# A four-layer conditioned stack on one core: the setup stage is spread over the first attention and the gate stage, and the norms of two attentions move one step

## What is computed

```python
# layer 0: 16 heads of 64
mod = silu(c) @ W_mod + b_mod                 # six rows of 256 per sequence: shift, scale, gate, twice
x = x + g_msa * attention(layernorm(x) * (1 + sc_msa) + sh_msa)
x = x + g_mlp * (gelu(modulated(layernorm(x)) @ W1 + b1) @ W2 + b2)
# layer 1: 16 heads of 16; rmsnorm, q and k normed and rotated by positions, SwiGLU
mod = c @ ada_w.T + ada_b
# layer 2: 16 heads of 16; layernorm, rotary, gelu MLP, then a gate:
mod = silu(c) @ film_w.T + film_b
x = x + gelu(v_) * tanh(g_) @ tg_out_w.T + tg_out_b
# layer 3: low-rank weights made from the condition
h = gelu(layernorm(c) @ W1 + b1)              # 64 x 256
w = h @ W2 + b2                               # 64 x 8192: four factors of 256 x 8 per sequence
y = gelu((x @ a1) @ bb1.T); out = x + (y @ a2) @ bb2.T
```

## Time and profile before

| what | value |
|---|---|
| time, median of 3 runs | 2367.48 us (2367.0 to 2367.68) |
| the profiled execution: its own time / its span | 2364.86 us / 2363.1 us |
| PE busy | 2005.7 us (85%) |
| DVE busy | 1455.1 us (62%) |
| ACT, POOL busy | 968.7 us (41%), 835.4 us (35%) |
| mean granted TensorE clock | 0.946 of full |

### The profile page before, as it was taken

The page is one execution under the profiler, slowest core; times in us unless marked ns, Lnnn a source line. Parts: engine busy times, 40 slices in busy tenths (PEclk is TensorE's granted clock), DMA queues, the critical chain, the costliest instruction groups (busy, mean ns, idle before and its releaser), DMA issues. The chain is left out here.

```text
span 2363.1 us, 41380 instructions
## 1 busy us (share of the span) xinstructions
PE 2005.7 (85%) x15274; PEld 1565.9 (66%) x15274; DVE 1455.1 (62%) x2120; ACT 968.7 (41%) x1594; POOL 835.4 (35%) x759
## 2 busy tenths in 40 slices
PE   4829999999999799867787679997877877998998
PEld 4618878878887577646565567774655656777775
DVE  1236655656566455468888856775777774554554
ACT  0024434434444566534454433332333345664332
POOL 0041111211011344456665723345656572443000
PEclk9959999999999999978999989998998999999999
DMA  7120000000000100010000000001000000000001
GB/s 301 55 74 2 2 2 1 1 2 1 1 1 10 49 0 0 0 41 2 0 0 0 1 25 0 0 1 36 1 0 0 0 2 27 0 0 32 5 0 72
DMA packets 19519, 44.28 MB, mean 19 GB/s; under 512 B 3200, under 2 KB 11200, under 8 KB 18176
## 3 DMA queue, kind: packets, MB, share of 16 engines
q1 hardware_dynamic: 19392, 42.48, 5.1%
HBM read 36.18 MB, written 6.29 MB: 18 GB/s over the span
## 5 line engine op out<-in xcount | busy, mean ns | idle before, releaser
L1223 DVE TENSOR_TENSOR Glb<-Gfb,Ghb 128x512 fp32r<-128x512 f32 x176 | 168.2, 964 | 101.6 <-ACT Ghb L1176 100.0
L523 POOL TENSOR_TENSOR Tm<-Dv,MOD 128x512 f32<-128x512 f32 x96 | 111.3, 1179 | 298.6 <-DVE Dv L580 208.0
L633 PE MATMUL bank<-HH,W1b 128*128 128x512 f32 x448 | 183.8, 410 | 13.2 <-PEq L1493 6.9
L633 PE MATMUL O<-Ghb,W2b 128*128 128x512 f32 x352 | 144.1, 409 | 54.0 <-DVE Glb L1223 52.4
L634 PE MATMUL bank<-HL,W1b 128*128 128x512 f32 x448 | 177.2, 396 | 0.0
L635 PE MATMUL bank<-HH,W1b 128*128 128x512 f32 x448 | 176.9, 395 | 0.0
L1378 PE MATMUL bank<-WQKa,HH 128*128 128x512 f32 x256 | 101.4, 483 | 78.3 <-DVE HL L588 63.6
L653 POOL TENSOR_TENSOR spare<-RT 128x1 f32<-128x1 f32 x48 | 9.5, 197 | 446.0 <-DVE RT L644 446.0
L512 POOL TENSOR_TENSOR XS<-Tm 128x512 f32<-128x512 f32 x48 | 70.5, 1469 | 245.6 <-ACT Tm L478 245.6
L635 PE MATMUL O<-Ghb,W2b 128*128 128x512 f32 x352 | 138.4, 393 | 0.0
L634 PE MATMUL O<-Glb,W2b 128*128 128x512 f32 x352 | 137.8, 392 | 0.0
(11 more groups left out here) (244 smaller groups left out, 5470.0 us busy)
## 6 DMA issues: line engine op xcount, KB each, us to landing
w<-l_w_dram SPq DMA_DIRECT2D x4, 2048.0 KB, 26.7
wm<-w_mods_dram SPq DMA_DIRECT2D x6, 768.0 KB, 12.1
X<-xT_dram SPq DMA_DIRECT2D x4, 1024.0 KB, 36.3
out_dram<-XO SPq DMA_DIRECT2D x8, 512.0 KB, 2.7
W2b_f<-l_w_dram SPq DMA_DIRECT2D x11, 256.0 KB, 5.0
WQK_f<-l_wqk_dram SPq DMA_DIRECT2D x8, 256.0 KB, 7.1
W1b_0f<-l_w_dram SPq DMA_DIRECT2D x8, 256.0 KB, 3.5
b2r<-l_b2r_dram SPq DMA_DIRECT2D x1, 1024.0 KB, 7.7
```

The source lines that it names most:

```text
L523: nc.gpsimd.tensor_tensor(Tm[:, k].rearrange("p (b t) -> p b t", t=T), Dv[:, k].rearrange("p (b t) -> p b t", t=T), m, ALU.mult).then_inc( ...
L633: nc.tensor.matmul(out, w_lo_ap, x_hi, start=first, stop=False)
L1223: nc.vector.tensor_tensor(Gl[m % gb][:], gf, Gh[m % gb][:].bitcast(F32), ALU.subtract).then_inc(g_lo.h, 1)
```

## The change

1. **The setup block is gone.** Constants, x (chunk by chunk) and the modulation weights (one layer at a time, in one buffer) are loaded in the block of attention 0. Layer 0's modulation is made there as before, between the norms of chunks 0 and 1. Layers 1 and 2 are made with the condition as the stationary side: two halves of 64 sequences side by side, then a copy (ACT), transposes (PE) and the store (DVE), around the first two steps.
2. **The low-rank weights are made in the gate block** (`Hyper`): in chunks 0 to 4, after the steps m = 1 and m = 3, a slot of work is put into the lists of PE, ACT and DVE. SP loads the low-rank weights in 8 parts of 1 MB, writes the factors out and only then reads them back. The gate's chunks are all written out, without a loop.
3. **attention12**: each part of the norm of chunk c + 2 moves to an earlier step of chunk c.

```diff
--- before.py
+++ after.py
 attention0, sync:
+                        for out, src in small:
+                            sp.dma_start(out, src).then_inc(d_in.h, 16)
+                        x_chunk(sp, 0)
+                        mod_weights(sp, 0)
+                        x_chunk(sp, 1)
                         st.weights.load(sp, 0)
...
                         st.weights.load(sp, 1)
+                        x_chunk(sp, 2)
+                        sp.wait_ge(m_ps.h, m_ps.at(2))
+                        mod_weights(sp, 1)
                         st.weights.load(sp, 2)
+                        x_chunk(sp, 3)
+                        sp.wait_ge(m_ps.h, m_ps.at(3))
+                        mod_weights(sp, 2)
+                        for c in range(4, NCH):
+                            x_chunk(sp, c)
 attention0, tensor:
+                def mod_products(pe, l):
+                    pe.wait_ge(m_w.h, m_w.at(32 * (l + 1)))
+                    for k in range(DH):
+                        for n in range(2):
+                            nc.tensor.matmul(O2[n * B:(n + 1) * B, 0, :], (cT if l == 1 else cS)[:, k, :], wm[:, k, n * 512:(n + 1) * 512],
+                                             start=(k == 0), stop=(k == DH - 1), skip_group_check=True)
+                    for k in range(DH):
+                        last = nc.tensor.matmul(O2[0:B, 1, :], (cT if l == 1 else cS)[:, k, :], wm[:, k, 1024:1536],
+                                                start=(k == 0), stop=(k == DH - 1), skip_group_check=True)
+                    last.then_inc(m_ps.h, 1)
...
+                        step(0, 0, 0, 2, first=True)
+                        mod_transposes(pe, 1)
+                        pe.wait_ge(m_done.h, m_done.at(6))
+                        mod_products(pe, 2)
+                        step(0, 1, 0, 2, first=True)
+                        mod_transposes(pe, 2)
+                        st.weights.ready(pe, st.weights.all())
                         chunks(pe, steps(step, lambda c: None))
 feed_forward, gate:
+                        if hyper:
+                            hyper.sync(sp)
                         nxt.loads(sp)
...
                                 last.then_inc(g_used.h, 1)
+                                if hyper:
+                                    hyper.tensor(pe, c, m)
...
-                        chunks(pe, body)
+                        chunks(pe, body, gate)
 class Hyper, tensor:
+                    for k in range(DH):
+                        for q in range(2):
+                            last = nc.tensor.matmul(S2[q * B:(q + 1) * B, 0, :], self.hT[:, k, :], self.W2[n % 3][:, q, k],
+                                                    start=(k == 0), stop=(k == DH - 1), skip_group_check=True)
 class Hyper, scalar (slots 2 to 5; slots 0 and 1 have a sqrt, a copy and two gelus):
+                    act.wait_ge(l3_ps.h, l3_ps.at(n + 1))
+                    nc.scalar.activation(self.AsT[n % 2][:], S2[:, 0, :], ACT.Copy).then_inc(l3_cp.h, 1)
 attention12, scalar:
-                            if t == (1 if more else 3):
-                                f, cc, pp = late(fr, nf, c, p, more)
-                                f.act_hh(act, cc, pp)
-                            if more and t == 3:
-                                f, cc = early(fr, nf, c, more)
-                                f.act_sqh(act, cc)
...
+                            f, cc = early(fr, nf, c - 1 if tail else c, more)
+                            if t == 1:
                                 f.act_square(act, cc)
-                            if more == 2 and tail:
-                                fr.act_rstd(act, c + 1)
+                            if t == 2:
+                                f.act_sqh(act, cc)
+                            if t == 3 and more:
+                                f.act_rstd(act, cc)
+                            if tail and more:
+                                f.act_hh(act, cc, 1 - p)
 attention12, gpsimd:
+                            if t == 1:
+                                f.pool_ss(pool, cc)
+                            if t == 2:
+                                f.pool_sql(pool, cc)
                             if t == 3 and more:
-                                f.pool_sql(pool, cc)
-                            if more == 2 and t == 0:
-                                fr.pool_h(pool, c + 1, 1 - p)
+                                f.pool_h(pool, cc, p)
```

More of the change, by code:

```diff
@@ L621, in x_there, with x_loaded, chunks @@
             pass
-        def chunks(eng, body):
+        def x_loaded(eng, c):
+            if isinstance(c, int) and c < 2:
+                eng.wait_ge(x_in[c].h, x_in[c].at(16 * DH))
+        def chunks(eng, body, unrolled=False):
+            if unrolled:
+                for c in range(NCH):
+                    body(c, c % 2, 2 if c < NCH - 2 else NCH - 1 - c)
+                return
             with eng.Fori(0, NCH // 2 - 1) as j:
@@ L814, in _ @@
-                        pe.wait_ge(d_in.h, d_in.at(16))
+                        pe.wait_ge(c_set.h, c_set.at(2))
+                        fr.pe_mean(pe, 0)
+                        pe.wait_ge(f_d.h, fr.at(f_d, 1))
+                        fr.pe_var(pe, 0)
+                        pe.wait_ge(m_w.h, m_w.at(32))
+                        pe.wait_ge(c_sil.h, c_sil.at(1))
+                        for h in range(2):
+                            for m in range(6 * h, 6 * h + 6):
+                                for k in range(DH):
+                                    last = nc.tensor.matmul(BK[h][:, (m % 6) * B:(m % 6) * B + B], wm[:, k, m * P:(m + 1) * P], cS[:, k, :],
+                                                            start=(k == 0), stop=(k == DH - 1))
+                            last.then_inc(m_ps.h, 1)
@@ L938, in step @@
                                 wt.high(act, 4 if j == 0 else wt.all())
-                        for j in range(2):
-                            step(0, j, 0, 2, first=True)
+                        mod_copy(act, 1)
+                        step(0, 0, 0, 2, first=True)
+                        st.weights.high(act, 4)
+                        mod_copy(act, 2)
+                        step(0, 1, 0, 2, first=True)
                         chunks(act, steps(step, lambda c: None))
@@ L1202, in body @@
                                     wt.high(act, 1)
-                        chunks(act, body)
+                        chunks(act, body, gate)
                     @block.vector
@@ L1258, in body @@
                                 residual_dve(dve, c, l, G_M, bcol_out, O2)
-                        chunks(dve, body)
+                        chunks(dve, body, gate)
                     @block.gpsimd
@@ L1748, in step @@
                                 ol(tt - 1, prev)
[L1749 to L1752 removed]
+                            f, cc = early(fr, nf, c - 1 if tail else c, more)
+                            if t == 1:
+                                f.dve_d(dve, cc)
+                            if t == 3 and more:
+                                f.dve_norm(dve, cc)
+                            if tail and more:
+                                f.dve_hl(dve, cc, 1 - p)
                         def residual(c, more):
```

519 lines of the change are left out of this document (265 added, 254 removed).

## The result

| | before | changed |
|---|---|---|
| median of 4 runs | 2367.24 us | 2256.68 us (2252.96 to 2259.85) |
| ratio, 95% interval | | 0.9532 [0.951, 0.9554] |
| profiled execution: own time / span | 2364.86 / 2363.1 us | 2252.96 / 2251.1 us |
| PE busy, mean granted clock | 2005.7 us, 0.946 | 1965.9 us, 0.957 |

What follows compares the result with a forecast made beforehand. By stage, PE was taken to bound the gate and nothing in the middle attentions, where it waited 63.6 us for HL. 2364.9 - 111 + 34 - 50 = 2238, plus 2.6 for the median: 2240 us, range 2210 to 2276.

Steps and rivals of the forecast that it cites:

- Term 1: Head of the program, up to attention 0's third step of heads: removing the serial prelude saves 111 us (bounds 104 to 116).
- three main points: Head: DVE and ACT start at 13.3 us, first projection at 44.8, third step of heads at 78.
- The price of half-products side by side: Modulation products of layers 1 and 2: halves run together, 0.93 us per 512-column product, 3.7 us per layer.
- Term 2: Gate: low-rank weight slots add 19.4 us of PE work and 14.6 of waits, +34 us (bounds 24 to 52).
- The rule on weight loads: Gate: loads overlap products only for another row group, so column halves run one after the other: +52, total 2258.
- the row: Profile row of line 736: 64 half-records in 3.71 us, so halves run together; gate +34, total 2240.
- Term 3: Attentions of layers 1 and 2: moving norm parts earlier removes PE's wait for HL, -50 us (bounds 26 to 70).
- about 39.3, so 3.2 a chunk: Layer 1's attention: a turn falls from 42.5 to about 39.3 us, a gain of 3.2 us per chunk.
- The first rival: Attentions: DVE's later output tile makes PE idle in the tail instead; gain 0 to 10 us, total about 2285; 8%.
- cost 2 in each layer: First chunk of layers 1 and 2: DVE stands still for chunk 1's HL where PE did, costing 2 us each.
- DVE and POOL stop each other: Attentions: modulation, norm, HL and residual, moved together, each could lose 1 us; 42 us less gain, total 2282; 7%.
- Feed-forward 2 and low rank: Feed-forwards and low-rank layer: unchanged, so 0 us difference.

Runs made afterwards that it cites:

- part 3 alone: Kernel before with only the attention of layers 1 and 2 as changed, setup and gate as before: 2337.35 us, ratio 0.9869.
- the fastest kernel: Changed kernel with gate slots one step later, first norm earlier in both layers, tile chain first in layer 2 only: 2209.02 us, ratio 0.9334.

## Why the prediction was right, and where it was not

The measured median lies inside the range, with the forecast's sign and 87% of its size (110.6 of 127.5). Two of the three terms held for the reasons given; the third held in layer 2 and failed in layer 1.

- **Term 1, head, -111: right** within 1 us at its three main points (13.3, 44.8 and 78 forecast, 13.24, 44.60 and 77.80 measured), with some luck between the first two. The difference from the mean started at 19.73, not near 18.0, and the modulation products ended at 36.9, not 35.7; from there to the first projection it took 7.7 us instead of 9.1. The price of half-products side by side held: 3.6 us for six products, forecast 3.7.
- **Term 2, gate, +34: right in sum, +32.5**, with two sizes off against each other: waits 9.3 instead of 14.6, and 3.8 us of slower products that the sum did not have (it took the clock as 1.00; it was 0.96). The run with the slots later shows that the added waits are those that the text named, ACT and DVE doing the slot first: without that they fell to 7.9 us, where the kernel before had 7.3.
- **The rule on weight loads**, which the prediction takes from the page TensorE: Matmul & The Clock Gate of the Trainium skill (What overlaps and what doesn't), would by its reading have put the gate at +52. Slots at 1.94 us for four products decide for the row; issued half by half they took the same.
- **Term 3, attentions, -50: the step that failed**, -35 (and -30 with part 3 alone), inside its bounds of 26 and 70. Layer 2 was about right: -27.4 in this profile and -24 on average of six, for about -29, and its turn of 37.5 came out step by step. Its working holds two slips, though: 9.9 against 8.0 is 1.9 us, not 1.7, and 42.3 less 37.5 is 4.8 a chunk, of which 4.4 was taken without a reason; the six turns gained 4.1 each, since the last of them gained only 0.9. In layer 1 the step "about 39.3, so 3.2 a chunk" was mis-sized: 40.95, so 1.5 a chunk in the loop. That is 7 of the 14 us; the first chunk (5.8 longer instead of 2) and the last (1.0 shorter instead of 4.5) are the rest. The sum took a turn as steps of DVE's and PE's work, and the tile as the only thing that comes late; layer 1 also has the q-k norm, a round trip from DVE to ACT to PE in every step, and PE's longest wait in the tail (3.66 us) is now at its end. But neither that chain nor the norm's place is shown to be what sets the turn: with the copies ahead of the root the turn grew to 42.4, and with the norm all but taken away it stayed at 41.
- **The first rival, the wait that only changes place**, came true in layer 1 by its effect (PE's idle time 94.0, then 97.1), not by its mechanism: the wait there is for PTa, the output tile is 0.67 us late, and the clock rose. What was gained in layer 1 is clock.
- **First chunk, "cost 2 in each layer"**: DVE did stand still for HL (5.4 us in layer 2), and PE's wait there was 8.6 us in layer 2 and 11.0 in layer 1. Doing that norm ahead of the first step gave back 8.8 and 3.3.
- **DVE and POOL stop each other** (7%): the price was real but not where I looked. HL, 2.23 us before, takes 1.83 at its new place in a turn of layer 2 (1.23 alone). The q-k norm's small instructions pay instead. In the changed kernel the one of line 1380 takes 0.18 us at the least and 0.65 in the median (below); 30 of its 32 executions overlap a POOL instruction, and each of these ends 35 to 41 ns after that instruction does. The section that the prediction named in the Trainium skill, SBUF - State Buffer (Who interferes with whom), counts among the DVE instructions that exclude POOL's those with two SBUF inputs and scalar ones in a two-port mode; the rows agree. Line 1380 is a scalar one with one input.
- **Feed-forward 2 and low rank**: forecast 0, measured +4.3, with a lower clock in both. The run with part 3 alone has nearly the same (+3.8), so it isn't the new gate. The low-rank layer varies by itself, though: it took 38.0 us with the copies before the root and 35.9 in the fastest kernel, both with part 3. What makes it vary is open.

The instruction of line 1380 in the changed kernel (min/median/max in ns, first and last start):

```profile
L1380 DVE TENSOR_SCALAR SSa<-SSa x32: 180/653/1589, 905.1 to 1230.0; 128x32 f32<-128x32 f32 x32
```

What stays open: what sets layer 1's turn at 41 us, and why its clock follows the arrangement so closely. The tile chain first and the shrunk norm shortened PE's idle time there, and both lost it again to a lower granted clock; only the first chunk's edit did not. The rows of the shrunk norm show where (behind the tile's wait and at t = 3), but no run changed the clock alone. In layer 2 the tile chain first went with a higher clock (0.93, then 0.94 to 0.98).

## What to carry to other kernels

Forecast each variant of a stage from its own timeline: the layer with one more round trip between engines (here the q-k norm) did not behave like its neighbour. When something is moved ahead on an in-order engine, move its whole chain: in layer 2 the tile alone gave nothing (324.7 us), the tile with its copy on the next engine over 20 us (303.4). And compare stages by idle and busy time of PE apart, since an edit can win the one and lose the other by the clock.

## What was not expected of the hardware

Products that fill 64 output rows each run beside those of the other 64 rows even when a whole product pair of one half is ahead in the list (slot 1.94 us in both orders). A DVE instruction on 32 columns lasts anything from 0.18 to 1.97 us, by how much of a POOL instruction is still to come: in 30 of 32 cases of line 1380 it ends some 0.04 us behind that. And 10 us less idle time of PE in one stage came with 10 us more busy time for the same products, at clock 0.88 instead of 0.91.
